# Overwriting the sorted rows with pad rows early, by copies inside DRAM, in a two-pass mixture-of-experts kernel

## The chip, the cores and the metric

The kernel runs on one core of a Trainium2 chip. The core has TensorE (PE), VectorE (DVE), ScalarE (ACT), GpSimd (POOL) and SyncE (SP), each with its own instruction queue, and 16 DMA engines that all queues share. SP's and ACT's transfers are issued by hardware queues of their own (q1 and q10 in the profile), POOL's by a software queue (q0). The metric is device time in microseconds (us).

## The reference

The input x is 2 x 1024 rows of 128 numbers. Three layers with residuals, the first and the last the same mixture-of-experts feed-forward with the same weights:

```python
x = x + 0.5 * ffn(layernorm(x))
x = x + attn(layernorm(x))      # projections, short convolutions, delta rule, gate, output
x = x + 0.5 * ffn(layernorm(x))

def ffn(x):                     # 8 experts, each token goes to one
    pb = softmax(xf @ gate_w + gate_b)
    weights = pb * (one-hot of the largest)
    for e in range(8):
        h = gelu(xf @ w1[e] + b1[e])
        out += weights[:, e] * (h @ w2[e] + b2[e])
```

## The kernel before

The program is a row of blocks: the first feed-forward (`moe_ffn`, rep 0), the attention layer in three blocks (`attn_project`, `attn_delta`, `attn_mix`), and the second feed-forward (`moe_ffn`, rep 1). Each block gives every engine its list of work, in the order in which it is written; all engines meet at a barrier at the block's end, SP too.

A feed-forward sorts the 2,048 tokens by expert. `xsort` is a tensor in DRAM with eight regions of CAP = 16 x 128 + 128 = 2,176 rows, one for each expert, and 128 rows behind them; a row is 258 floats (1,032 bytes): the normalised token, its number, its weight, and the row that the result is added to. The 128 rows behind the regions hold pad rows: zeros, with a token number of 2,048, which the final scatter drops.

DVE and PE work out each token's expert and its rank in it, in four chunks of four tiles, and with them the row `pos`. POOL then scatters each tile of `xr` to `xsort` with an indirect DMA (L201), 16 of them. An expert's tokens don't fill its last tile of 128 rows, so pad rows must stand behind them. `store_pads` does that: when all the counts are known, DVE copies them to `padrow` (L448), and SP (even experts) and ACT (odd experts) each read four of them into a register (L153) and store the 128-row tile `pad` behind the last token (L154). POOL makes `pad` (L190 to L192). In the first feed-forward `lead["store_pad"]` also stores one pad tile behind the regions (L1937).

SP waits for all scatters and all pads and then loads the 23 sorted tiles in turn, each from a row that it reads from `row0` (L177, L178):

```python
sp.wait_ge(scattered, 16 * NT)
sp.wait_ge(pads_in, 16 * NE)
```

PE turns a tile (`turn_rows`, L273), multiplies it by the first weights (`up`, L282) and the second (`down`, L292); ACT copies and applies gelu (L346, L354), DVE copies the expert's weights to `w1s` (L475) and takes the result (L486), POOL scatters it (L208). Before its loop ACT copies the biases into the weights (L340), and it does so behind its pad stores.

In the projection block neither SP nor ACT issues a transfer, and SP has no work at all. In the mixing block SP issues 16 loads: four pieces of `m_wpair` (L1374) and twelve of `m_pairs` (L1378 to L1380), which PE's gate waits for (L1426): the first ten of them for the first half of the sequence. In the second feed-forward SP first issues the two loads of the weights (L162, L163).

Of the kernel before, what the change touches and what calls it, by code (L numbers as in the profile page):

```python
# [6 lines left out]
I32 = mybir.dt.int32  # L7
# [40 lines left out]
def moe_ffn(nc, rep, cst, mem, banks, NT, NE, F, lead=None):  # L48
# [19 lines left out]
    with ExitStack() as ctx:  # L68
# [87 lines left out]
        with nc.Block() as block:  # L156

            @block.sync
            def _(sp):
                if rep == 0:  # L160
                    lead["load_x"](sp)
                sp.dma_start(W1[:, :, 0:F], a["L0_ffn_w1"].rearrange("e d f -> d e f")).then_inc(weights_in, 16)  # L162
                sp.dma_start(W2[:], a["L0_ffn_w2"].rearrange("e (j f) d -> f e j d", f=P)).then_inc(weights_in, 16)  # L163
                if rep == 0:
                    sp.wait_ge(pad_made, 1)
                    lead["store_pad"](sp, pad)
                store_pads(sp, range(0, NE, 2))

                sp.wait_ge(row0_ready, 1)
                first_rows = [sp.value_load(row0[0:1, t:t + 1], min_val=0, max_val=NE * CAP) for t in range(2)]  # L170
                sp.wait_ge(scattered, 16 * NT)
                sp.wait_ge(pads_in, 16 * NE)
                if rep == 0:
                    sp.wait_ge(mem["pad_stored"], 16)
                for c, (g, n) in enumerate(LOADS):
                    for t in range(g, g + n):
                        r = first_rows[t] if t < 2 else sp.value_load(row0[0:1, t:t + 1], min_val=0, max_val=NE * CAP)  # L177
                        sp.dma_start(xs[:, t, :], xsort[bass.ds(r, P), :]).then_inc(x_loaded[c], 16)  # L178
                if rep == 0:
                    lead["load_attn"](sp)  # L180

                sp.wait_ge(y_stored, 16 * MAXT)
                if not last:
                    xnext = mem["xnext"].rearrange("(t p) d -> p t d", p=P)
                    for c in range(NC):
                        sp.dma_start(X[:, tiles(c), :], xnext[:, tiles(c), :]).then_inc(mem["x_back"][c], 16)

            @block.gpsimd
            def _(gp):
                gp.memset(pad[:, 0:D], 0.0)  # L190
                gp.memset(pad[:, D:D + 1].bitcast(I32), NT * P)
                gp.memset(pad[:, D + 1:WIDE], 0.0).then_inc(pad_made, 1)  # L192
                if rep == 0:
                    lead["gpsimd"](gp)
                gp.iota(base[:, 0, :], [[CAP, NE]], base=0, channel_multiplier=0, allow_small_or_imprecise_dtypes=True).then_inc(ranks_read, 1)
                if rep == 0:
                    gp.wait_ge(mem["numbered"], 1)
                for c in range(NC):
                    gp.wait_ge(pos_ready, c + 1)
                    for t in range(c * CT, (c + 1) * CT):  # L200
                        gp.indirect_dma_start(xsort, bass.IndirectOffsetOnAxis(pos[:, t:t + 1], 0),  # L201
                                              xr[:, t, :], None).then_inc(scattered, 16)
                if rep == 0:
                    lead["make_masks"](gp)
                for t in range(MAXT):
                    gp.wait_ge(y_ready, t + 1)

                    gp.indirect_dma_start(mem["out"] if last else mem["xnext"], bass.IndirectOffsetOnAxis(row(t), 0), Y[:, t, :], None,  # L208
                                          bounds_check=NT * P - 1, oob_is_err=False).then_inc(y_stored, 16)
# [98 lines left out]
            @block.scalar  # L308
            def _(act):
                if rep == 0:  # L310
                    lead["scalar"](act)
                def root(c):
                    act.wait_ge(var_ready, c + 1)
                    act.activation(rstd[:, tiles(c)], vare[:, tiles(c)], ACT.Sqrt).then_inc(std_ready, 1)

                def copy_turned(c):
                    act.wait_ge(xnT_psum, c + 1)
                    act.activation(XNT[:, c * BANK:(c + 1) * BANK], pT[c % 2][:], ACT.Copy).then_inc(xnT_ready, 1)  # L318

                def exp(c):  # L320
                    act.wait_ge(shifted, c + 1)
                    act.activation(ex[:, tiles(c), :], lg[:, tiles(c), :], ACT.Exp).then_inc(exp_done, 1)

                root(0)
                copy_turned(0)
                root(1)
                exp(0)
                copy_turned(1)
                root(2)
                exp(1)  # L330
                copy_turned(2)
                root(3)
                exp(2)
                copy_turned(3)
                exp(3)
                store_pads(act, range(1, NE, 2))
                if rep == 0:
                    lead["take_bias"](act)
                act.wait_ge(mem["bias_ready"], 3)
                act.activation(W1[:, :, F:F + FC], b1T[:], ACT.Copy).then_inc(b1_ready, 1)  # L340
                if rep == 0:
                    lead["take_taps"](act, 0, 3)

                def copy_rows(t):
                    act.wait_ge(xT_psum, t + 1)
                    act.activation(xT[:, t, :], pX[t % 2][:, 0:P], ACT.Copy).then_inc(xT_ready, 1)  # L346

                def gelu(t):
                    act.wait_ge(h_psum, t + 1)
                    if t >= 2:  # L350

                        act.wait_ge(y_psum, t - 1)
                    for j in range(FC):
                        act.activation(hT[:, t % 2, j, :], pH[t % 2][:, j * P:(j + 1) * P], ACT.Gelu,  # L354
                                       bias=w1s[:, t % NB, F + j:F + j + 1]).then_inc(h_ready, 1)

                copy_rows(0)
                copy_rows(1)
                for t in range(MAXT):
                    gelu(t)  # L360
                    if t + 2 < MAXT:
                        copy_rows(t + 2)
                if rep == 0:
                    lead["take_products"](act)
                    act.wait_ge(var_ready, NC + 1)
                    act.activation(rstd[:], vare[:], ACT.Sqrt).then_inc(std_ready, 1)
                    lead["take_taps"](act, LASTQ, LASTQ + 1)

            @block.vector
            def _(ve):  # L370
# [74 lines left out]
                place(3)  # L445

                ve.wait_ge(ranks_read, NC + 1)
                ve.tensor_copy(padrow[:], base[:, NC, :]).then_inc(padrow_ready, 1)  # L448
                ch.step(ve.tensor_tensor(cnt[:], base[:, NC, :], base[:, 0, :], ALU.subtract))
                ch.step(ve.tensor_tensor(over[:], cnt[:].unsqueeze(2).to_broadcast([P, NE, NT]),  # L450
                                         cst["tilestart"][:, 0:NT].unsqueeze(1).to_broadcast([P, NE, NT]), ALU.is_gt))
# [76 lines left out]
def attn_project(nc, cst, mem, banks, B, L, NH, done):  # L528
# [7 lines left out]
    with ExitStack() as ctx:  # L536
# [37 lines left out]
            return ap.rearrange("p (t c) -> p t c", c=P)  # L574

        with nc.Block() as block:

            @block.tensor
            def _(pe):
# [1448 lines left out]
```

## Time and profile before

| | us |
|---|---|
| three runs | 508.62, 513.08, 515.13 |
| their median | 513.08 |
| the profiled execution, its time | 509.69 |
| its span, from first to last instruction | 507.7 |
| PE busy in it | 411.1 (81%) |
| DVE busy | 303.5 (60%) |
| ACT busy | 239.8 (47%) |
| POOL busy | 143.3 (28%) |
| moved by DMA | 30.31 MB |

A row of the timeline gives the start, the duration, the engine and the line, and in brackets how long the engine was idle before it and what released it; SPq and ACTq are the queues that issue transfers, and their duration is that of the issue. Landing times stand apart, in the chain of waits and in the list of issues. A packet is one piece of a transfer on one DMA engine.

### The profile page before, as it was taken

To read this page: it belongs to the slowest core of one execution; us is meant where nothing else is said; L and a number is where in the kernel's file an instruction comes from. 1 tells how busy PE (TensorE), PEld (TensorE's weight loads), DVE (VectorE), ACT (ScalarE), POOL (GpSimd) and SP (SyncE) were. 2 spreads that over 40 slices of the span, in tenths; PEclk is the share of its full clock that TensorE was granted. 3 is DMA by queue.
4 is the path that set the end of the run, shared out by engine and by line. 5 is a ranking of instruction groups with operands and counts; after the bars stand their busy time and mean duration, and the time that the engine had idled before them with its cause. 6 is when DMAs were issued, how large, how long until landed. Compare 5 with 4: busy or idle time off the path is not lost. (4 is left out here: it accounts for less than half of the span.)

```text
span 507.7 us, 13213 instructions
## 1 busy us (share of the span) xinstructions
PE 411.1 (81%) x5049; PEld 327.3 (64%) x5049; DVE 303.5 (60%) x818; ACT 239.8 (47%) x511; POOL 143.3 (28%) x172
## 2 busy tenths in 40 slices
PE   2756999979987989889999999965999537329995
PEld 1655999766566877667777666752445426319994
DVE  5943455367684588778765555462278867714551
ACT  2605676466681587976421000052655336116763
POOL 4467355400002396030100000030024203713553
PEclk9999999969896599999999999997898555558998
DMA  7726442120000000000000000038000019344400
GB/s 258 222 95 156 132 126 63 44 67 1 1 0 4 4 4 4 6 4 4 2 3 1 0 1 1 3 74 196 1 0 1 1 44 327 128 126 133 118 32 4
DMA packets 27388, 30.31 MB, mean 60 GB/s; under 512 B 7670, under 2 KB 20899, under 8 KB 27328
## 3 DMA queue, kind: packets, MB, share of 16 engines
q1 hardware_dynamic: 22672, 22.04, 16.0%
q0 software_dynamic: 3008, 6.34, 3.8%
q10 hardware_dynamic: 1648, 1.10, 0.8%
q8 instruction: 41, 0.67, 0.5%
q14 instruction: 19, 0.16, 0.1%
HBM read 17.48 MB, written 9.49 MB: 53 GB/s over the span
## 5 line engine op out<-in xcount | busy, mean ns | idle before, releaser
L354 ACT ACTIVATE hT<-bank,w1s 128x128 f32<-128x128 f32 x184 | 52.5, 368 | 27.4 <-PE bank L282 27.4
L282 PE MATMUL bank<-xT,w1s 128*128 128x128 f32 x368 | 52.4, 289 | 0.6 <-ACT xT L346 0.6
L292 PE MATMUL bank<-W,hT 128*128 x368 | 50.2, 281 | 0.8 <-ACT hT L354 0.8
L282 PEld LDWEIGHTS bank<-xT,w1s 128*128 128x128 f32 x368 | 48.1, 204 | 1.1 <-ACT xT L346 1.0
L292 PEld LDWEIGHTS bank<-W,hT 128*128 128x128 f32 x368 | 46.3, 198 | 1.2 <-issue 1.2
L1240 DVE TENSOR_TENSOR d_BD<-bank,quarter 128x2048 f32<-128x2048 f32 x16 | 36.6, 2289 | 11.3 <-PE bank L890 11.3
L475 DVE COPY w1s<-W 128x516 f32 x46 | 20.6, 450 | 36.4 <-issue 29.1
L1102 ACT ACTIVATE d_BD<-d_TP 32x512 f32<-32x512 f32 x64 | 40.5, 633 | 0.9
L201 POOL DMA_INDIRECT xsort<-xr,pos x32 | 31.5, 984 | 32.9 <-DVE pos L424 24.4
L208 POOL DMA_INDIRECT out<-Y,xs x23 | 22.6, 983 | 35.2 <-issue 18.7
L486 DVE SCALAR_TENSOR_TENSOR Y<-bank,xs 128x128 f32<-128x128 f32 x46 | 16.2, 351 | 27.0 <-PE bank L292 17.9
L208 POOL DMA_INDIRECT xnext<-Y,xs x23 | 22.6, 982 | 25.9 <-issue 18.9
L1573 POOL TENSOR_TENSOR m_DSQ<-DEL 128x512 f32<-128x512 f32 x4 | 4.1, 1039 | 91.4 <-POOLq L897 89.9
L1294 DVE TENSOR_TENSOR d_TT<-bank,blk 128x128 f32<-128x128 f32 x64 | 16.5, 292 | 18.1 <-PE bank L1039 18.1
L273 PE MATMUL bank<-ident,xs 128*128 128x128 f32 x46 | 13.5, 298 | 15.4 <-DMA xs<-xsort 15.2
L1139 ACT ACTIVATE d_TMP<-bank 128x512 f32<-128x512 f32 x4 | 2.4, 597 | 48.7 <-PE bank L1073 48.7
L220 PE MATMUL bank<-ident,xr 128*128 128x128 f32 x32 | 9.9, 464 | 17.8 <-DVE xr L384 16.4
L1024 PE MATMUL bank<-d_TT,KBT 128*32 128x128 f32 x128 | 20.1, 279 | 4.6 <-DVE d_TT L1294 3.7
L890 PE MATMUL bank<-d_BD,d_ATP 128*32 128x128 f32 x512 | 18.4, 287 | 5.2 <-ACT d_BD L1102 5.2
L1039 PE MATMUL bank<-xr,K 32*128 32x128 f32 x128 | 22.6, 296 | 0.0
L1289 DVE TENSOR_TENSOR xr<-xr,bank 32x128 f32<-32x128 f32 x64 | 16.2, 284 | 10.2 <-PE bank L1024 10.2
L1580 POOL TENSOR_TENSOR m_PM<-DEL,m_ex 128x512 f32<-128x512 f32 x4 | 6.3, 1578 | 51.8 <-DVE m_ex L1633 51.8
(298 smaller groups left out, 967.0 us busy)
## 6 DMA issues: line engine op xcount, KB each, us to landing
xs<-xsort SPq DMA_DIRECT2D x46, 129.0 KB, 2.1
W<-in_L_ffn_w SPq DMA_DIRECT2D x2, 2048.0 KB
xsort<-pad SPq DMA_DIRECT2D x9, 129.0 KB
xsort<-pad ACTq DMA_DIRECT2D x8, 129.0 KB
xr<-in_L_attn_x SPq DMA_DIRECT2D x4, 256.0 KB, 5.1
xr<-xnext SPq DMA_DIRECT2D x4, 256.0 KB, 3.9
m_pairs<-FS SPq DMA_DIRECT2D x4, 256.0 KB, 5.0
m_pairs<-firT SPq DMA_DIRECT2D x4, 256.0 KB, 4.9
```

What stands on the lines that cost most here:

```text
L201: gp.indirect_dma_start(xsort, bass.IndirectOffsetOnAxis(pos[:, t:t + 1], 0), xr[:, t, :], None).then_inc(scattered, 16)
L208: gp.indirect_dma_start(mem["out"] if last else mem["xnext"], bass.IndirectOffsetOnAxis(row(t), 0), Y[:, t, :], None, bounds_check=NT * P ...
L282: mm = pe.matmul(pH[t % 2][:, j * P:(j + 1) * P], w1s[:, t % NB, j * P:(j + 1) * P], xT[:, t, :], start=True, stop=True)
L292: mm = pe.matmul(pY[t % 2][:, 0:D], hT[:, t % 2, j, :], W2[:, bass.ds(e, 1), j, :], start=(j == 0), stop=(j == FC - 1))
L354: act.activation(hT[:, t % 2, j, :], pH[t % 2][:, j * P:(j + 1) * P], ACT.Gelu, bias=w1s[:, t % NB, F + j:F + j + 1]).then_inc(h_ready, 1)
L475: ve.tensor_copy(w1s[:, t % NB, :], W1[:, bass.ds(experts[t], 1), :]).then_inc(staged, 1)
L890: mm = pe.matmul(bank[a * C:(a + 1) * C, t * P:(t + 1) * P], lhs(t, a), BD[:, slot, t * NH + a, :], start=True, stop=True)
L1024: pe.matmul(banks[b][c * C:(c + 1) * C, 0:P], WT[:, cols], SB[:, b, :], start=True, stop=True).then_inc(ws_psum, 1)
L1039: pe.matmul(banks[2 + b][:, 0:P], K[rows, tile, :], U[rows, tile, :], start=(n == 0), stop=(n == STEPS_S - 1), skip_group_check=True).then ...
L1102: cp = act.activation(spread_dst(i % 2, a), blocks(TP[a * C:(a + 1) * C, i % NG, :]), ACT.Copy)
L1240: ve.tensor_tensor(BD[:, 2 + i % 2, :, :].rearrange("p s (a n) -> p s a n", n=C), all_blocks(banks[i % 2][:]), mask, ALU.mult).then_inc(z_ ...
L1294: ve.tensor_tensor(SB[:, b, :], banks[2 + b][:, 0:P], cst["blk"][:], ALU.mult).then_inc(s_ready, 1)
```

## The change

In the second feed-forward no pads are stored behind the counts, `pad` is not made again and `padrow` is not written. Instead SP issues eight copies in the projection block. Each overwrites one expert's region of 2,176 rows with the 128 pad rows that stand behind the regions, 17 times over. Their completion counts on `pad_stored`, and POOL waits for all of it before its first scatter in the second feed-forward. The code views a region as 17 x 16 pieces of 8 rows.

```diff
@@ moe_ffn, sync
-                store_pads(sp, range(0, NE, 2))
+                if rep == 0:
+                    store_pads(sp, range(0, NE, 2))
...
                 sp.wait_ge(scattered, 16 * NT)
-                sp.wait_ge(pads_in, 16 * NE)
                 if rep == 0:
+                    sp.wait_ge(pads_in, 16 * NE)
                     sp.wait_ge(mem["pad_stored"], 16)
@@ moe_ffn, gpsimd
-                gp.memset(pad[:, 0:D], 0.0)
-                gp.memset(pad[:, D:D + 1].bitcast(I32), NT * P)
-                gp.memset(pad[:, D + 1:WIDE], 0.0).then_inc(pad_made, 1)
                 if rep == 0:
+                    gp.memset(pad[:, 0:D], 0.0)
+                    gp.memset(pad[:, D:D + 1].bitcast(I32), NT * P)
+                    gp.memset(pad[:, D + 1:WIDE], 0.0).then_inc(pad_made, 1)
                     lead["gpsimd"](gp)
...
+                if rep == 1:
+                    gp.wait_ge(mem["pad_stored"], 16 + 16 * NE)
                 for c in range(NC):
@@ moe_ffn, scalar
-                store_pads(act, range(1, NE, 2))
                 if rep == 0:
+                    store_pads(act, range(1, NE, 2))
                     lead["take_bias"](act)
@@ moe_ffn, vector
-                ve.tensor_copy(padrow[:], base[:, NC, :]).then_inc(padrow_ready, 1)
+                if rep == 0:
+                    ve.tensor_copy(padrow[:], base[:, NC, :]).then_inc(padrow_ready, 1)
@@ attn_project, a block of its own for sync
+            @block.sync
+            def _(sp):
+                xsort, cap = mem["xsort"], NT * P + P
+                n = xsort.shape[0] // cap
+
+                def pieces(ap):
+                    return ap.rearrange("(a b) w -> a (b w)", b=8)
+
+                empty = pieces(xsort[n * cap:n * cap + P, :])
+                for e in range(n):
+                    sp.dma_start(xsort[e * cap:(e + 1) * cap, :].rearrange("(n a b) w -> n a (b w)", b=8, a=P // 8),
+                                 empty.unsqueeze(0).to_broadcast([cap // P] + list(empty.shape))).then_inc(mem["pad_stored"], 16)
```

On SP, the order of the program before from the end of the first feed-forward to the mixing stage's loads (the line, the operation, the tensors, the shape that the instruction carries):

```order
L156 UNCONDITIONAL_BRANCH
L1369 UNCONDITIONAL_BRANCH
L1374 DMA m_wpair<-wbr 64x2x128 x4
L1378 DMA m_pairs<-FS 64x1024
L1379 DMA m_pairs<-firT 64x1024
L1380 DMA m_pairs<-VP 64x1024
```

The same place of the program after, whose line numbers are 12 to 17 higher:

```order
L156 UNCONDITIONAL_BRANCH
L582 UNCONDITIONAL_BRANCH
L592 DMA xsort<-xsort 17x3x11008 x8
L580 UNCONDITIONAL_BRANCH
L1386 UNCONDITIONAL_BRANCH
L1391 DMA m_wpair<-wbr 64x2x128 x4
L1395 DMA m_pairs<-FS 64x1024
L1396 DMA m_pairs<-firT 64x1024
L1397 DMA m_pairs<-VP 64x1024
```

The eight copies stand ahead of the mixing stage's loads in the same queue, and the shape of each is 17 x 3 x 11,008 floats: the sixteen pieces of 8 rows, which lie one behind the other, stand as three pieces of 44,032 bytes.

On SP in the second feed-forward, the program before, from the weights to the first sorted tile:

```order
L162 DMA W_1<-in_L_ffn_w 128x8x512
L163 DMA W_1<-in_L_ffn_w 128x32x128
L153 TENSOR_LOAD padrow
L153 ISA x2
L154 ISA
L154 DMA xsort<-pad 128x258
```

```order
L170 TENSOR_LOAD row_1
L170 ISA x2
L170 TENSOR_LOAD row_1
L170 ISA x2
L178 ISA
L178 DMA xs<-xsort 128x258
```

And after:

```order
L162 DMA W_1<-in_L_ffn_w 128x8x512
L163 DMA W_1<-in_L_ffn_w 128x32x128
L171 TENSOR_LOAD row_1
L171 ISA x2
L171 TENSOR_LOAD row_1
L171 ISA x2
L179 ISA
L179 DMA xs<-xsort 128x258
```

The four pad stores with their register loads are gone between the weights and the first sorted tile.

## Rows read from the trace of the kernel before

**Rows 1.** The page: the span, and DMA busy share in 40 slices, in tenths.

```profile
span 507.7 us, 13213 instructions
...
DMA  7726442120000000000000000038000019344400
```

**Rows 2.** Waits of SP's queue in the whole span: waiting line, releaser, us, times, longest.

```profile
SPq L897 <- PEq L897: 180.9, 1, 180.9
SPq L1367 <- PEq L1367: 64.3, 1, 64.3
SPq L576 <- PEq L576: 43.6, 1, 43.6
```

**Rows 3.** Timeline: start us, us, engine, line, operation, count, idle before and its releaser.

```profile
110.88 0.09 DVE L752 MEMSET a_PRE<- 128x6 f32 x2 [0.97 <-PEq L156]
...
347.90 2.04 PE L1426 MATMUL bank<-XNT,w1x 128*128 128x512 f32 x2 [5.81 <-DMA m_pairs<-VP]
```

**Rows 4.** Chain that ended last, second feed-forward: start us, us, what.

```profile
449.71 2.10 DMA xsort<-pad
...
452.57 2.16 DMA xs<-xsort
```

**Rows 5.** Timeline around the head of the second feed-forward's loop.

```profile
445.48 0.96 POOL L201 DMA_INDIRECT xsort<-xr,pos  x1 [0.30 <-issue]
...
448.93 0.23 ACT L340 ACTIVATE W<-b1T 128x32 f32<-128x32 f32 x1 [11.73 <-issue]
450.37 0.43 DVE L475 COPY w1s<-W 128x516 f32 x1 [6.86 <-issue]
```

**Rows 6.** Queue and issues of ACT: queue, packets; out<-in, count, KB each.

```profile
q10 hardware_dynamic: 1648, 1.10, 0.8%
...
xsort<-pad ACTq DMA_DIRECT2D x8, 129.0 KB
...
gw<-in_L_ffn_gate_w ACTq DMA_DIRECT2D x1, 4.0 KB
gb<-in_L_ffn_gate_b ACTq DMA_DIRECT2D x1, 4.0 KB
b1rows<-in_L_ffn_b ACTq DMA_DIRECT2D x1, 16.0 KB
b2rows<-in_L_ffn_b ACTq DMA_DIRECT2D x1, 4.0 KB
c_firp<-in_L_attn_fir_l ACTq DMA_DIRECT2D x1, 15.5 KB, 5.4
```

**Rows 7.** Windows: stretch us, busy of each engine, clock, DMA share, GB/s.

```profile
0.00:16.74 16.74, 6.96 (x28) 5.87 (x28) 10.11 (x52) 6.22 (x10) 6.22 (x27) 1.00 0.86 267
...
421.00:423.00 2.00, 1.37 (x5) 0.85 (x5) 1.86 (x10) 0.40 (x2) 0.00 (x0) 0.50 1.05 401
423.00:425.00 2.00, 2.00 (x10) 2.00 (x11) 1.41 (x10) 1.95 (x4) 0.00 (x0) 0.50 1.06 305
...
449.00:451.00 2.00, 0.00 (x0) 0.00 (x0) 0.43 (x1) 0.16 (x1) 0.00 (x0) 0.50 0.58 198
```

**Rows 8.** DMA issues of the mixing stage: count, KB each, us to landing.

```profile
m_pairs<-FS SPq DMA_DIRECT2D x4, 256.0 KB, 5.0
m_pairs<-firT SPq DMA_DIRECT2D x4, 256.0 KB, 4.9
m_pairs<-VP SPq DMA_DIRECT2D x4, 256.0 KB, 5.1
...
m_wpair<-wbr SPq DMA_DIRECT2D x4, 64.0 KB, 2.1
```

**Rows 9.** Timeline of SP's queue at the start of the kernel.

```profile
3.69 2.47 SPq L163 DMA_DIRECT2D W<-in_L_ffn_w  x1
6.21 10.53 SPq L1937 DMA_DIRECT2D xsort<-pad  x1
```

## The prediction

> **What bounds the kernel now.** I read the page first: a span of 507.7 us, and a DMA row that is 7 to 9 tenths busy at both ends and nearly 0 in the middle [rows 1]. Then the waits of SP's queue, because the change puts work there. SP waits 43.6 us in the projection, 180.9 us in the delta stage and 64.3 us in the mixing stage [rows 2]; with the first instruction of the projection at 110.88 us [rows 3] these make stage borders of about 110.9, 154.5 and 335.4 us. So during 225 us neither SP nor the DMA engines have anything to do, and copies that the DMA engines finish in that time would be free. Last I read the chain that ended last, at the second feed-forward. PE's first transpose there waits for the first load of a sorted tile, and that load waits for the last pad store: the store takes 2.10 us from 449.71 (landing 451.81), the load 2.16 us from 452.57 [rows 4]. Behind it PE runs 23 tiles without a gap to the end. Only that short head can be gained.
>
> **Removed: the pads behind the counts.** The second feed-forward loses 4 pad stores on SP and 4 on ACT, the copy of `padrow`, 3 memsets on POOL, and SP's wait on `pads_in`. What SP waits for next is `scattered`. POOL's last scatter stands at 445.48 and takes 0.96 us, so it is issued at 446.44 [rows 5]. No row shows when a scatter has landed; the nearest is the pad store's 2.10 us, a write of the same tensor, and I take it: 448.54. Before, SP went on at 451.81, so it gains 3.3 us. The bounds: 5.4 us if a scatter landed at once, nothing if it takes as long as 5.4 us. The other two things that PE's first tile needs don't take the place of the load. ACT's copy of the biases (L340, 448.93) stood behind ACT's own four stores and moves ahead with them, and DVE's first `w1s` copy (450.37) was behind that [rows 5]. The memsets and the `padrow` copy cost nothing on the path: POOL is idle then until its first scatter, and DVE has nothing late in front of it. The loop itself is unchanged. **-3.3 us.**
>
> **Added: eight copies inside DRAM.** Each writes 17 x 128 rows of 1,032 bytes, that is 2.246 MB; eight make 17.97 MB. What decides is how many DMA engines share them. The order list gives their shape as 17 x 3 x 11008: the 16 pieces that the code asks for have been merged again, and the outer dimension is 17. What the trace tells of outer dimensions: ACT's queue issued thirteen transfers: `gw`, `gb`, `c_firp` and eight pads with 128 rows each, `b1rows` with 32 and `b2rows` with 8 [rows 6]. Their rows sum to 11 x 128 + 32 + 8 = 1,448 packets; the queue's row says 1,648. The other 200 are 12 x 16 + 8. I read that as one closing packet on each engine that a transfer uses: sixteen engines for every transfer whose outer dimension is a multiple of 16, eight for the one with 8 rows. All are equal shares. Seventeen can't be cut into equal shares over 2 to 16 engines, so my forecast is that each copy runs on **one** engine, and all eight on the same one. Rows alone leave the other reading open (rows dealt out in turn, the seventeenth to the first engine again), for no transfer here has an outer dimension above 16 that isn't a multiple of 16.
>
> The Trainium skill ("DMA: Bandwidth & Descriptors", section on why a DMA increments its semaphore by 16 and not by 1) decides between the two: the engine count is the largest number up to 16 that divides the slowest dimension of both sides, and on these queues it is the lowest-numbered engines that are used. By that rule the count here is 1 and the time is that of the forecast; by rows dealt in turn it would be that of the first rival below. No run so far shows a 17.
>
> The price on one engine. When the weights stream in 2 KB rows, all sixteen move 401 GB/s [rows 7], 25.1 GB/s each. 17.97 MB at 25.1 GB/s are **717 us**, from 110.9 to 827.6 us. The trace has no copy inside DRAM, so bounds: the same weights in 512-byte rows move at 305 GB/s or less, and the pads at 198 GB/s with 0.58 of the engines busy, 21.3 GB/s for a busy one [rows 7], which gives 843 us. The other way: 512 bytes at 305/16 GB/s take 26.9 ns, 2,048 at 25.1 take 81.7 ns; the straight line through these goes at 28.0 GB/s for long pieces, 642 us. I take 25.1, the rate that was seen.
>
> **What waits for it.** Two things. POOL's first scatter of the second feed-forward now waits for `pad_stored` at 144. But something earlier does: the 16 loads of the mixing stage (4 `m_wpair` of 64 KB, 12 `m_pairs` of 256 KB [rows 8]) go through SP's queue too, and on the first engine their share stands behind the copies. PE's first gate matmul (L1426, 347.90) is the one that waits for them [rows 3]. Ahead of it are 4 x 64 KB and 6 x 256 KB; a sixteenth is 0.11 MB, 4.6 us at 25.1 GB/s. It then starts at 827.6 + 4.6 = 832.2 instead of 347.9: **+484.3 us**. POOL's wait has by then been over, so it adds nothing.
>
> **Does SP itself get stuck?** It must hand over all eight before the barrier at the projection's end. SP's issue of the first pad store took from 6.21 to 16.74 us [rows 9]. The delta stage then runs 180.9 us to 754, still ahead of 827.6: it is hidden under the last 145 pieces, and the mixing stage waits for its loads. The other queues (instruction fetches, the scatters) are nearly idle in that time.
>
> **Sum:** 507.7 + 484.3 - 3.3 = 988.7 us of span; with the 2.0 us that the profiled execution's own time (509.69) has around its span, **991 us**. The median of the runs before, 513.08, is 3.4 us above that execution.
>
> **The rivals.**
> (1) The copies are spread over all engines, so the kernel isn't slower. For it: the 8-row transfer is as well explained by dealing rows in turn. At 401 GB/s the eight take 45 us; with the seventeenth row on one engine 2/17 of 17.97 MB at 25.1 GB/s is 84 us, to 195 us, and both are over long before 335.4. Only -3.3 us is left: 506 us. That is also what it would be with eight or more engines in use; the point from which it decides is 335.4 - 110.9 = 224.5 us, reached with 717 / 224.5 = 3.2 engines. Chance 0.17.
> (2) One engine, and the delta stage is not hidden. If the 44,032-byte pieces are cut to 4 KB, 94 of them are only 0.39 MB. The eighth copy is taken at 110.9 + 7 x 89.6 - 15.4 = 723 us, the delta stage ends at 904, and the rest follows: 904 - 335.4 = +568.6, or 1,075 us in all. At the slower rate of 21.3 GB/s (105.4 us a copy) the same working gives 1,183; without the cutting it is 953.9 + 5.4 - 347.9 = +611, 1,118 us. For it: no packet of SP's queue so far is as long as 8 KB. Against it: the shape itself was cut to 44,032 bytes. Chance 0.20.
> (3) The change doesn't do what it says: SP's wait was not the pads' but the scatters'. Then the head gains nothing, 3.3 us more in either case. It changes no chance.
>
> **How the numbers follow.** One engine with the delta stage hidden: 0.63; (2) 0.20; (1) 0.17. Faster by over 2% needs 10 us, which the head of the second feed-forward doesn't hold: 0.01. Within 2% (what a measurement of this kernel can tell from no change): 0.16. Slower: 0.83. The range starts at the fast line, 642 us in place of 717, 915 us, and ends at (2) with the slower rate, 1,185 rounded. The likeliest case's own range is 915 to 1,118.
>
> **What would show it.** Right: SP's wait in the projection vanishes while its eight issues last some 460 us; the mean DMA busy share is about 1/16 for some 700 us at 25 GB/s; the longest wait of PE is for `m_pairs` at L1426; the first tile load of the second feed-forward follows the last scatter. Wrong: 17.97 MB moved by 200 us at 200 GB/s or more, and a projection of 43.6 us as before. Then the reading of the 200 packets fails at 17, and everything behind it.

## The result: 940 us, and the profile after

| | before | after |
|---|---|---|
| median of the runs, us | 511.96 | 939.84 |
| the profiled execution, us | 509.69 | 939.81 |
| its span, us | 507.7 | 937.8 |

The median before is now that of four executions. The ratio is 1.833, with a 95% interval of 1.823 to 1.843 (that of the two medians is 1.836). Some executions of one kernel show a lower mean clock than others and are a few per cent longer; ratios and intervals in this document compare the faster ones alone. The forecast was 991 us, from 915 to 1,185. The kernel got slower by the mechanism that was put first, and 51 us less than it said.

The page of the kernel after, its span, the DMA row and the rate in 40 slices (it answers to [rows 1]), and the queue that holds SP's transfers:

```profile
span 937.8 us, 13167 instructions
...
PE   4599895000000000000006988999960006966497
...
DMA  8352100000000000000000000000011222006340
GB/s 248 127 136 72 52 27 27 28 26 28 26 28 26 28 26 26 28 26 28 26 28 29 30 33 30 30 27 30 27 39 37 58 60 64 1 0 201 108 121 17
...
q1 hardware_dynamic: 22512, 39.48, 12.9%
```

For fourteen slices of 23.4 us on end PE is idle, and all that time the DMA engines move 26 to 28 GB/s. Windows of the same execution (columns as in [rows 7]) give the mean, and the share of the sixteen engines that was busy:

```profile
113.00:500.00 387.00, 39.52 (x173) 23.86 (x172) 32.62 (x48) 28.89 (x44) 0.00 (x0) 0.55 0.06 27
500.00:690.00 190.00, 173.16 (x3626) 138.98 (x3627) 114.88 (x216) 72.47 (x118) 35.51 (x19) 0.88 0.07 30
...
776.00:777.00 1.00, 0.00 (x0) 0.00 (x0) 0.00 (x0) 0.00 (x0) 0.00 (x0) 0.50 1.00 194
```

0.06 of sixteen is one engine. The last of the copies' pieces is done at about 776 us; by then all sixteen engines are busy with the last of the mixing stage's loads. The queue's packets say the same in another way. Before there were 22,672 of them:

```profile
q1 hardware_dynamic: 22672, 22.04, 16.0%
```

The change takes 4 pad stores of 128 + 16 packets from SP's queue, which leaves 22,096, and there are 22,512: 416 more, or eight copies of 51 pieces and **one** closing packet each.

What waited (SP's queue first, as in [rows 2], then all engines):

```profile
SPq L914 <- PEq L914: 191.0, 1, 191.0
SPq L1384 <- PEq L1384: 72.2, 1, 72.2
...
SPq L580 <- PEq L580: 0.2, 1, 0.2
```

```profile
PE bank L926 <- PEq L580: 346.3, 1, 346.3
...
PE bank L1443 <- DMA m_pairs<-VP: 84.3, 1, 84.3
```

SP has no wait left in the projection (0.2 us, where there were 43.6). PE waits 346.3 us at the barrier in front of the delta stage, and 84.3 us in front of the gate. SP's queue from the timeline:

```profile
111.30 388.81 SPq L592 DMA_DIRECT2D xsort<-xsort  x8
691.92 10.44 SPq L1391 DMA_DIRECT2D m_wpair<-wbr  x4
...
703.05 25.28 SPq L1396 DMA_DIRECT2D m_pairs<-firT  x1
728.37 12.94 SPq L1397 DMA_DIRECT2D m_pairs<-VP  x1
```

```profile
782.91 2.05 PE L1443 MATMUL bank<-XNT,w1x 128*128 128x512 f32 x2 [84.34 <-DMA m_pairs<-VP]
```

```profile
880.32 1.07 POOL L204 DMA_INDIRECT xsort<-xr,pos  x1 [0.30 <-issue]
...
883.22 6.39 SPq L179 DMA_DIRECT2D xs<-xsort  x7
...
885.51 0.93 PE L276 MATMUL bank<-ident,xs 128*128 128x128 f32 x2 [11.62 <-DMA xs<-xsort]
```

The same places of the second feed-forward before:

```profile
415.24 0.38 SPq L162 DMA_DIRECT2D W<-in_L_ffn_w  x1
...
452.02 24.87 SPq L178 DMA_DIRECT2D xs<-xsort  x23
```

The gate starts at 782.91 in place of 347.90, +435.0 us. From the issue of the second feed-forward's weights to its first tile load are 32.9 us (850.29 to 883.22), before 36.8, and to the end 87.5, before 92.5. 507.7 + 435.0 - 5.0 = 937.7: the whole difference is accounted for.

### The profile page after: what moved, and what is told of

Read it like the earlier page. It is cut to its first block and busy times, and to the rows that moved or that the text cites. A ratio compares the mean times of both kernels' runs of the same rounds, so it can differ in the third digit from the quotient of the medians.

```text
span 937.8 us, 13167 instructions
## 1 busy us (share of the span) xinstructions
PE 421.7 (45%) x5049; PEld 334.4 (36%) x5049; DVE 304.2 (32%) x817; ACT 239.6 (26%) x511; POOL 143.4 (15%) x169
## 3 DMA queue, kind: packets, MB, share of 16 engines
q1 hardware_dynamic: 22512, 39.48, 12.9%
## 5 line engine op out<-in xcount | busy, mean ns | idle before, releaser
L926 PE MATMUL bank<-KBT,KT 32*32 32x32 f32 x512 | 8.2, 237 | 346.5 <-PEq L580 346.3
L926 PEld LDWEIGHTS bank<-KBT,KT 32*32 32x32 f32 x512 | 7.5, 150 | 346.9 <-issue 346.8
L1213 DVE TENSOR_TENSOR d_TMP<-d_ATP,t2mask 128x512 f32<-128x512 f32 x4 | 2.8, 692 | 353.3 <-ACT d_ATP L1111 353.3
L1111 ACT ACTIVATE d_ATP<-bank 128x512 f32<-128x512 f32 x4 | 2.4, 597 | 358.8 <-PE bank L926 358.8
L1160 POOL MEMSET d_BD<- 128x4096 f32 x1 | 3.5, 3511 | 401.5 <-SPq L914 401.5
L1443 PE MATMUL bank<-XNT,w1x 128*128 128x512 f32 x16 | 10.5, 744 | 84.3 <-DMA m_pairs<-VP 84.3
L1443 PEld LDWEIGHTS bank<-XNT,w1x 128*128 128x128 f32 x16 | 2.9, 223 | 86.1 <-issue 86.1
L1610 DVE TENSOR_REDUCE ST<-m_FSt 128x16 f32<-128x512 f32 x4 | 2.7, 680 | 88.0 <-ACT m_FSt L1497 88.0
L1497 ACT ACTIVATE m_FSt<-bank 128x512 f32<-128x512 f32 x4 | 2.4, 590 | 91.3 <-PE bank L1410 91.2
## 6 DMA issues: line engine op xcount, KB each, us to landing
m_pairs<-firT SPq DMA_DIRECT2D x4, 256.0 KB, 16.7
```

The lines of the kernel that those rows point to most:

```text
L926: mm = pe.matmul(banks[6 + g % 2][h * C:(h + 1) * C, t * P + c * C:t * P + (c + 1) * C], KT[rows, cols], KBT[rows, cols], start=True, stop ...
L1443: pe.matmul(bank[:], cst["w1x"][:], XNT[:, cols], start=True, stop=False)
```

## The experiments

### Sixteen outermost

```diff
-                    return ap.rearrange("(a b) w -> a (b w)", b=8)
+                    return ap.rearrange("(a b) w -> a (b w)", a=16)
...
-                    sp.dma_start(xsort[...].rearrange("(n a b) w -> n a (b w)", b=8, a=P // 8),
-                                 empty.unsqueeze(0).to_broadcast([cap // P] + list(empty.shape))).then_inc(mem["pad_stored"], 16)
+                    sp.dma_start(xsort[...].rearrange("(n a b) w -> a n (b w)", n=cap // P, a=16),
+                                 empty.unsqueeze(1).to_broadcast([16, cap // P, empty.shape[1]])).then_inc(mem["pad_stored"], 16)
```

> The changed kernel with one thing different: each copy is viewed as 16 x 17 pieces of 8 rows (8,256 bytes), 16 outermost, instead of 17 x 3 pieces of 44,032 bytes. My theory (the DMA engines of a transfer are the largest number up to 16 that divides its outer dimension, so 17 gives one engine and 16 gives sixteen): 17.97 MB at 16 x 27.06 GB/s (the rate of one engine in the changed kernel: 408 pieces in 664 us) are 42 us, perhaps 90 if copies inside DRAM share a limit, over by about 155 to 200 us of the span, long before the mixing stage. SP isn't held, the gate waits for nothing, and only the head of the second feed-forward is left: 3.9 to 5.0 us less than before, a span of 502.7 to 503.8, a time near 505. The queue's packets grow to 22,096 + 8 x (16 x 17 + 16) = 24,400. Rival (the slowness lies in copies inside DRAM or in their number of bytes, not in the shape): 700 us or more. Rival (the copies disturb the projection's or the delta stage's own work): those stages longer than 43.6 and 180.9 us.

Measured: 516.39 us (509.20 to 523.28), a ratio to before of 1.0136 with an interval of 0.9993 to 1.028. The same bytes, the same place, the same number of transfers, and the time is 423 us shorter: it was the shape of the transfers alone. The order of the dimensions changed, and with it the length of a piece (8,256 bytes in place of 44,032); the versions with 34 and 68 outermost, both with pieces of 33,024 bytes, tell these two apart. The packets are 24,400, as expected.

```profile
PEclk9999999968975599999688999997988755557999
...
GB/s 263 205 156 112 140 101 74 83 198 322 327 316 224 4 4 4 4 5 4 1 2 1 1 1 1 1 8 203 54 0 1 1 0 294 142 103 133 101 31 4
...
q1 hardware_dynamic: 24400, 39.48, 25.1%
```

The copies run at 316 to 327 GB/s and are over in some 60 us. But it isn't the 505 us that I expected. The profiled execution (522.2 us) is one of the longer ones, and its delta stage takes 197.6 us, before 180.9. Windows of its beginning, and of the same stretch of the kernel before:

```profile
151.10:171.10 20.00, 10.45 (x402) 9.85 (x402) 4.19 (x6) 1.45 (x3) 3.51 (x1) 0.50 0.59 226
171.10:191.10 20.00, 19.61 (x612) 16.51 (x615) 14.72 (x16) 13.35 (x22) 13.22 (x7) 0.68 0.02 4
```

```profile
154.50:174.50 20.00, 17.30 (x580) 16.12 (x580) 8.49 (x13) 6.40 (x11) 5.34 (x2) 0.56 0.02 4
174.50:194.50 20.00, 18.02 (x698) 14.40 (x690) 17.14 (x14) 16.75 (x28) 19.29 (x11) 0.93 0.01 4
```

In the first 20 us of the stage PE gets 10.5 us of work done where it got 17.3, and the clock is still at its lower level for most of the next 20. What PE waited for there, in the kernel with 16 outermost and before:

```profile
PE bank L926 <- issue: 9.3, 3, 7.3
```

```profile
PE bank L909 <- issue: 2.2, 1, 2.2
```

It waited for nothing that the profile shows ("issue"; I read it as waiting for its own instructions), once for 7.3 us, while the last of the copies kept the DMA engines 0.59 busy in that window. This is a cost that I had put at nothing; see the last two experiments. It isn't all of the stage's 16.7 us. By the count of matmuls done, the stage is some 9 us behind after its first 40 us and 11 us after 60; the rest comes later, where the granted clock dips to 0.86, 0.80 and 0.91 in three windows of 20 us. The changed kernel, with one engine of copies, has such a dip too (0.79 and 0.70), and the kernel before has none in its profiled execution, so that part can't be put down to wide copies.

### The sixteen-wide copies, and the pads still stored

The same kernel, with the pads of the second feed-forward stored behind the counts as before (each of the two queues first waits for the copies; `pad`, `padrow` and the wait on `pads_in` are back too).

```diff
 moe_ffn, sync and scalar
-                if rep == 0:
-                    store_pads(...)
+                if rep == 1:
+                    eng.wait_ge(mem["pad_stored"], 16 + 16 * NE)
+                store_pads(...)
```

> One part alone: the sixteen-wide copies are made in the projection, and the second feed-forward still stores its pads behind the counts, as before. Theory: the copies cost nothing where they are, so this is the time of the kernel before within 1 us, and all of the gain of the kernel without pads comes from their absence. Rival (copies slow the attention stages by their traffic): some us slower than before.

Measured: 519.88 us (511.38 to 526.21), ratio 1.0178, interval 0.9964 to 1.0393. Not settled within 1 us; what can be read is the stages. The head of the second feed-forward is 35.9 us from weights to first tile load, with the pads gone 33.4. The delta stage takes 197.5 us, without the pads 197.6, and PE has "issue" waits here too in its first 60 us (8.3 us; without the pads 10.8, before 3.1). So the pads' absence gives back 2.5 to 3.9 us at the head (the second from the changed kernel against the kernel before), and the delta stage beside or behind the copies was longer by more than that in both profiled executions, which are both among the longer ones of their kernels.

### Thirty-four outermost

```diff
-                empty = pieces(xsort[n * cap:n * cap + P, :])
+                empty = xsort[n * cap:n * cap + 64, :].rearrange("r w -> (r w)")
...
+                    sp.dma_start(xsort[...].rearrange("(n r) w -> n (r w)", r=64),
+                                 empty.unsqueeze(0).to_broadcast([cap // 64, empty.shape[0]])).then_inc(mem["pad_stored"], 16)
```

> Each copy as 34 x 2 pieces of 33,024 bytes, 34 outermost. Theory (largest divisor up to 16): 34 gives two engines. 8.98 MB on each at 27.06 GB/s are 332 us, from 111.3 to 443.6. About 118 pieces were outstanding on the engine when the changed kernel's eighth copy was taken; with 34 pieces per engine and copy the eighth is taken after 7 x 34 - 118 = 120 pieces of 1.22 us, at 258 us, so the delta stage starts then instead of at 154.5, ends at 439 to 449, and the gate's loads land by 450 to 462: span 605 to 617, time 607 to 619. The queue's closing packets: 2 a copy, so 22,096 + 8 x (68 + 2) = 22,656. Rival (rows are dealt out in turn and 17 was one engine for some other cause): 16 engines, about 505 us, 22,096 + 8 x (68 + 16) = 22,768 packets.

Measured: 683.35 us, a span of 681.3.

```profile
GB/s 271 149 142 145 73 87 32 55 54 54 54 54 54 54 54 54 54 54 55 58 58 57 59 58 54 52 1 1 0 2 152 50 0 1 25 271 102 139 69 11
...
q1 hardware_dynamic: 22656, 39.48, 18.1%
```

```profile
107.50 212.16 SPq L589 DMA_DIRECT2D xsort<-xsort  x8
513.52 2.67 SPq L1388 DMA_DIRECT2D m_wpair<-wbr  x4
```

Two engines it is: 54 GB/s, twice one engine's, and 22,656 packets, two closing ones a copy. Rows dealt out over sixteen engines are excluded, with 17 and with 34. The time is 64 us above the upper end of what I expected (619 us), and the timeline shows why: SP was held for 212 us, not some 150. The delta stage starts at 319.7, ends 194 us later at 513.5, and there the loads find an empty queue. 513.5 - 335.4 = +178.1, less 4.1 for the second feed-forward: 681.7.

### Sixty-eight outermost

```diff
-                empty = xsort[n * cap:n * cap + 64, :].rearrange("r w -> (r w)")
+                empty = xsort[n * cap:n * cap + 32, :].rearrange("r w -> (r w)")
```

This is against the version with 34; the destination has `r=32`.

> Each copy as 68 pieces of 33,024 bytes, 68 outermost. Theory (largest divisor up to 16): four engines, 4.49 MB on each, 166 us from 111.3 to 277. SP isn't held (17 pieces per engine and copy, seven copies are 119), and 277 is before the mixing stage at 335.4: about 505 us, since four engines are more than the 3.2 at which the copies begin to show. 22,096 + 8 x (68 + 4) = 22,672 packets. Rival (dealt over sixteen): the same time but 22,768 packets; so the packets tell, and the DMA busy share of about 4/16 for 166 us against 16/16 for 42 us.

Measured: 535.71 us, a span of 533.8.

```profile
GB/s 261 205 167 94 150 89 61 80 80 107 101 109 109 111 113 113 113 114 110 114 84 1 1 1 1 1 2 73 184 1 0 1 1 178 216 92 129 136 31 4
...
q1 hardware_dynamic: 22672, 39.48, 23.2%
```

```profile
108.45 69.44 SPq L589 DMA_DIRECT2D xsort<-xsort  x8
366.29 2.69 SPq L1388 DMA_DIRECT2D m_wpair<-wbr  x4
```

Four engines, 111 GB/s, 22,672 packets: right. The time was not (about 505 expected): SP was held for 69 us, so the projection ended at 177.9 instead of about 151. The copies were done before the mixing stage, as expected, and it still cost 27 us at a barrier.

### Four copies on one engine, four on sixteen

The first four copies keep 17 outermost, the other four have 16 outermost.

```diff
-                for e in range(n):
+                for e in range(n // 2):
...
+                for e in range(n // 2, n):
```

> Four copies as in the changed kernel (17 outermost) and then four with 16 outermost. This tells apart the two things that can hold the program: SP at the barrier, and the mixing stage's loads behind the copies. The first engine has 4 x 51 pieces of 44,032 bytes (332 us) and then 4 x 17 of 8,256 (21 us): it is done at 464 us. If only the loads' place in the queue mattered, the gate would start at 470 in place of 347.9: 507.7 + 122 - 5 + 2 = 627 us. If SP also stands at its eighth copy until no more than about 118 pieces are left on the first engine (255 - 118 = 137 pieces, 223 us), the projection's barrier opens at 334, the delta stage ends at 515 to 525 and the mixing stage runs from there: 682 to 694 us. Theory: the second.

Measured: 783.69 us, a span of 781.8.

```profile
107.61 57.64 SPq L592 DMA_DIRECT2D xsort<-xsort  x4
165.31 257.47 SPq L599 DMA_DIRECT2D xsort<-xsort  x4
614.46 2.66 SPq L1398 DMA_DIRECT2D m_wpair<-wbr  x4
```

The loads' place behind the copies alone would give 627 us; the measured time is 157 us above it, so the barrier decides here. It is also some 90 us above the 682 to 694 that I had expected with the barrier. SP hands over its eighth copy at 422.8. By then the first engine, busy from 109 us on, has done 313.8 / 1.62 = 194 of the 255 pieces that stand ahead of the eighth (1.62 us a piece: below): 61 are left, not the 118 of my expectation. With that the sum closes to 0.7 us: mixing stage at 614.5, +279.1, less 4.3 for the second feed-forward, 782.5, where the span is 781.8.

### The changed copies, and the pads still stored

The edit of the second experiment, on the changed kernel itself: 17 outermost, and

```diff
-                if rep == 0:
-                    store_pads(...)
+                if rep == 1:
+                    eng.wait_ge(mem["pad_stored"], 16 + 16 * NE)
+                store_pads(...)
```

> The changed kernel's copies, unchanged (17 outermost), and the second feed-forward still stores its pads behind the counts. Theory: all of the loss is the copies', and the pads' absence gave back 4 to 5 us, so this takes 939.8 + 5 = 945 us. Rival (the second feed-forward was shorter for another cause, the clock or the emptier DMA queues): 940.

Measured: 939.70 us, where I expected 945. It reads like the rival, the same time as the changed kernel, but isn't it. From the weights' issue to the end it takes 91.6 us, the changed kernel 87.5, before 92.5: the 4.1 us are there. The first feed-forward of this execution happened to be 3.3 us shorter (the copies start at 108.03, in the changed kernel at 111.30), and as everything hangs on the copies' end, that is taken off the total: 937.8 + 4.1 - 3.3 = 938.6, where the span is 937.9. The head alone: 36.5 us to the first tile load with pads, 32.9 without.

### The mixing stage's loads on ACT's queue

In outline:

```diff
 attn_mix: the loop over m_wpair and m_pairs moves from the sync block
-                        sp.dma_start(...)
 to the head of the scalar block
+                act.dma_start(...)
```

> The changed kernel's copies (17 outermost, SP's queue), but the sixteen loads of the mixing stage are issued by ACT, on its own queue. If the place behind the copies in one queue is what holds the gate, the loads now only take turns with the copies on the first engine. With one piece in turn the 56 pieces of the first ten loads there wait 1.63 us each, 91 us from 692: no gain, 940 us. With more than one piece in turn, the gate starts near 710, and the second feed-forward near 777, where its first scatter finds the copies done: 860 to 870 us. If the gate waited for something else (POOL, the barrier), 940 as well, but then with the loads landed early. ACT spends some 12 us on the issues.

Measured: 935.59 us.

```profile
776.72 2.05 PE L1430 MATMUL bank<-XNT,w1x 128*128 128x512 f32 x2 [53.13 <-DMA m_pairs<-VP]
```

```profile
DMA to landing us min/median/max: 4.2/6.1/86.7
```

The gate starts at 776.72, 670 us after the first copy, in the changed kernel 672. The copies start 4.6 us earlier here (106.66), which is the 4 us of the total. The slowest load takes 86.7 us to land: it is the tenth of those that the gate waits for, issued at 689.85. The median of 6.1 us doesn't say that half of the loads were complete so early. The ten share one semaphore, and each adds 16 to it. If that is one from each of its sixteen closing packets, fifteen engines that are done with all ten make a count of 150, which passes the 144 of nine loads, and only the tenth shows when the first engine has done its shares. That the copies were nearly over by then (their end lies a few microseconds before) would leave two readings, but the packets decide: from 722 to 770 us SP's queue moves 28 of them and ACT's queue 28, and nothing else moves. The shared engine takes one piece of each queue in turn, a 1.6 us piece of a copy for each small one of a load (my estimate by that was 91 us). So another queue doesn't help, and the question which of the two, the queue or the engine, holds the loads has this answer: the engine is enough. The other fifteen engines had done their shares of the ten long before: the DMA busy share is 0.99 from 692 to 696 us and 0.05 from 704 to 708. What the gate's start would be with loads that keep off the copies' engine wasn't run.

### Four engines, in two blocks

All copies are viewed as `"(n a b) w -> a n (b w)"` with `a=4`. In outline:

```diff
 attn_project, sync
+                for e in range(0, 4):
 attn_delta, a block for sync
+                for e in range(4, 8):
```

> A version that could beat both: 4 outermost in each copy, so four DMA engines, with four of the copies issued in the projection block and the other four in the delta block. With 68 pieces outstanding on an engine when the next pair of copies is taken (seen in every run so far), four copies of 17 pieces hand over at once, so no barrier waits; 8 x 20.8 us of copying end by about 111 + 83 and 152 + 83 + some, long before the mixing stage; and twelve of the sixteen engines stay free for instruction fetches. Theory: projection 43 us, delta stage as before (181 to 186 us), second feed-forward 3.3 us shorter at its head; about 3 us faster than the kernel before of the same rounds, which is less than its own spread (501 to 519 us in the last rounds). Rival (any copy traffic beside the delta stage costs time): a delta stage of 190 us or more and no gain.

Measured: 510.87 us (505.98 to 519.08), a ratio of 1.0015 with an interval of 0.9964 to 1.0065: no difference that can be measured. The projection is about 44 us again and no barrier waits:

```profile
107.91 2.85 SPq L592 DMA_DIRECT2D xsort<-xsort  x4
151.96 24.95 SPq L926 DMA_DIRECT2D xsort<-xsort  x4
346.94 2.67 SPq L1405 DMA_DIRECT2D m_wpair<-wbr  x4
```

The delta stage of the profiled execution (518.07 us, one of the longest of twelve) takes 195 us, where I expected 181 to 186 and the rival 190 or more. Its "issue" waits in the first 60 us are 4.5 us, 1.4 us more than before. By the count of matmuls the stage is some 3 us behind after 60 to 80 us; the other 11 come later, where the granted clock falls to 0.79 and 0.67 in two windows of 20 us (before it stayed at 1.00). Whether the copies have a part in that dip isn't shown. The best version of this change thus gives about what it costs.

### Sixteen-wide copies beside the delta stage

In outline:

```diff
 attn_project
-            @block.sync: the eight copies
 attn_delta
+            @block.sync: the eight copies, with a=16 outermost
```

> The sixteen-wide copies, all eight issued in the delta block instead of the projection. In the kernel with 16 outermost, the copies still ran for the first 17 us of the delta stage; PE stood there 7.3 and 1.8 us for nothing but its own instructions, the clock rose at 184 instead of 177 us, and the stage took 197.6 us instead of 180.9. Theory (the fetches of PE's instructions wait behind the copies on the same DMA engines, and that keeps the clock low): with all of the 58 us of copying beside PE's 3,600 short matmuls the stage takes 25 to 45 us longer than 180.9, the span is 530 to 550 us, and PE's stalls put down to issue lie all in the first 60 us of the stage. Rival (the longer stage is the clock's own wandering from run to run): 181 to 198 us.

Measured: 541.05 us, a span of 539.2, a delta stage of 220 us.

```profile
152.00:172.00 20.00, 10.97 (x447) 10.32 (x433) 6.29 (x9) 1.79 (x3) 2.76 (x1) 0.55 0.85 312
172.00:192.00 20.00, 10.79 (x254) 8.60 (x255) 7.39 (x7) 9.32 (x15) 12.54 (x7) 0.67 0.85 317
192.00:212.00 20.00, 14.09 (x333) 10.35 (x336) 8.52 (x9) 8.77 (x15) 13.07 (x6) 0.67 0.73 275
```

```profile
PE bank L927 <- issue: 12.5, 3, 4.5
PE bank L894 <- issue: 8.5, 3, 4.1
PE bank L967 <- issue: 2.9, 1, 2.9
```

PE's "issue" waits in the first 60 us of the stage are 23.9 us, before 3.1. The clock rises and falls with them: in windows of 2 us it is at 1.00 from 182 to 184, from 188 to 190 and from 200 to 204, each time PE then stands idle (0.00 busy in 182:184, 190:192 and 204:206), and the clock is back at 0.50 by 186, 192 and 206. Only when the copies have gone, from 212 us, does it stay up for 40 us. The stage lost 39 us: by the count of matmuls some 26 in its first 60 us, beside the copies, and the rest later, most of it in the dip of the stage's middle (0.78, 0.63 and 0.83), which the changed kernel has too. The rival, wandering of the clock alone, would have ended at 198.

### Eight outermost

```diff
-                    return ap.rearrange("(a b) w -> a (b w)", b=8)
+                    return ap.rearrange("(a b) w -> a (b w)", a=8)
```

The destination is viewed as in the first experiment, with `a=8`.

> Eight outermost, all copies in the projection: 2.25 MB on each of eight engines, 83 us at 27.06 GB/s, so from 108 to 191 us. SP takes the eighth copy when 68 of 119 pieces of 0.61 us are left, after 31 us: no barrier waits. 22,096 + 8 x (136 + 8) = 23,248 packets. Theory of the fetches: a fetch waits only if it is on one of the eight busy engines, so the delta stage's first 40 us lose less than the sixteen-wide kernel's first 17: a stage of 183 to 192 us, a span of 507 to 516. Rival (fetches wait wherever copies run): the stage takes over 200 us, since the copies lie beside it for 40 us instead of 17.

Measured: 519.30 us, a span of 517.3, a delta stage of 198.1 us.

```profile
GB/s 266 205 164 105 150 95 74 83 102 207 215 215 216 213 212 27 4 4 5 1 2 1 1 0 1 2 1 154 112 0 1 1 0 226 192 101 126 133 31 4
...
q1 hardware_dynamic: 23248, 39.48, 23.9%
```

Eight engines, 215 GB/s, 23,248 packets. On the stage it is between my two readings. PE's "issue" waits in the stage's first 60 us, over all runs:

| copies beside them | "issue" waits, us |
|---|---|
| none (before) | 3.1 |
| one engine (changed kernel, its version with pads, loads on ACT) | 1.7, 2.4, 3.5 |
| two engines | 3.0 |
| four engines | 4.5, 4.9 |
| sixteen for 8 us, then one (four copies on each) | 7.1 |
| eight for 40 us | 9.6 |
| sixteen for 17 us (without and with pads) | 10.8, 8.3 |
| sixteen for 60 us | 23.9 |

The version with four copies on one engine and four on sixteen shows both in one execution: one wait of 5.1 us while the DMA engines are 0.76 to 0.79 busy, and 2.0 us in all in the rest of the 60, when one engine is left. So wide traffic makes PE wait, and traffic on one to four engines hardly does. That it is the fetch of PE's instructions that waits is my reading, and isn't shown. In the first 60 us of its delta stage the sixteen-wide kernel of the experiment above moved 8 packets through the instruction queue (q8), and they took 0.9% of the engines' time, 1.1 us for each; in the kernel before there were 15 in 1.6%, 1.0 us for each. So a fetch that is under way is hardly slower, and the wait would have to lie in front of it, where no row looks.

## Why the prediction was right, point by point

**One engine.** Right, and shown by six shapes: outer dimensions 17, 34, 68, 8 and 16 gave 1, 2, 4, 8 and 16 closing packets a copy, and rates of 27, 54, 111, 215 and some 320 GB/s. The outer dimension 4 of the split version closes with 4 as well (111 GB/s). The step that was least sure in the prediction, from an 8-row transfer to one with 17, holds; rival (1) is excluded for this shape. The Trainium skill's rule ("DMA: Bandwidth & Descriptors", why a DMA increments its semaphore by 16 and not by 1) named 1 for 17, and the trace agrees, as it does in every run with another shape.

**The price.** The mechanism was right and the size was off: 717 us, measured 665 (111.3 to about 776). The issues of the eight copies, as the trace lists them (min, median and max in ns):

```profile
L592 SPq DMA_DIRECT2D xsort<-xsort x8: 627/724/164885, 111.3 to 499.5; - x8
```

The longest, 164.9 us, is the time of exactly two copies, 4.491 MB: 27.2 GB/s for one engine, where I had taken 25.1 from the weights' 2 KB rows. The straight line through the two row sizes, which I used as a bound only, said 28.0. For pieces of 44 KB the line was the better guess: 1.62 us each instead of 1.76. This term made the forecast 52 us too high; the others nearly cancel (0.4 us for the start, 2.3 for the loads, 1.7 the other way for the second feed-forward).

**The loads.** Right. 4.6 us forecast between the copies' end and the gate, measured about 7.

**The hold of SP.** The mechanism was right, the term was not. I had one threshold: the next transfer is taken when 94 pieces are left. The trace shows steps: in the changed kernel the copies are taken in pairs, two at once, a third after 55 us and a fourth with it, then two more after 165 us and again after 165 us. At each step about 68 pieces are left on the engine from the copies taken before, and the eighth is taken with the seventh, at 500.1 instead of 573. In the changed kernel this changed nothing (the delta stage was hidden either way, and PE then waited 84 us for the gate). It misled me in three expectations: I had replaced 94 by 118 from the same trace, counting the eighth as if it had been taken alone. With 34 pieces a copy about 65 were left at the eighth, in the mixed kernel 61. What exactly a ring holds, and why the first pads of the program waited for 94 small rows, stays open.

**The delta stage** took 191.0 us, forecast 180.9. The time went to the clock: beside a single engine of copies PE's "issue" waits were no longer than before, but the granted clock fell to 0.79 and 0.70 in two windows in its middle. It cost nothing here. By the count of matmuls 1 us of the 10 was lost in the first 60 us and the rest in that dip; the same copies with the pads stored had a stage of 185.4 us, so it is no fixed price of the copies.

**The head of the second feed-forward.** Right: forecast -3.3 us. In nine kernels without the pads the first tile load is issued 32.9 to 33.4 us after the weights (mean 33.1), in the three with them 35.9 to 36.8 (mean 36.4). SP goes on 1.7 us after POOL is done with the last scatter (881.39 to 883.1), which I read as its landing, where I took 2.1. The other 1.1 us of the 5.0 in the changed kernel came behind the head; from run to run this part spreads from 54.6 to 58.1 us, about as much as the whole gain.

**The rivals.** (2) didn't come true: the pieces weren't cut to 4 KB (51 a copy by the packets), and the rate was above, not below. (3), the scatters holding SP instead of the pads, is excluded by the head.

**What I costed at nothing and wasn't.** Copies on many engines beside a stage of many short matmuls. The prediction called the fetches nearly idle and priced rival (1) at 506 us; the kernel that makes it true takes 516 in the median (its ratio to before lies between 0.9993 and 1.028, so no gain is shown and a small loss isn't excluded).

## What to carry to other kernels

Look at the shape that the instruction carries, not the one that the code wrote: here dimensions that lie one behind the other were merged, and an outermost broadcast of 17 put each transfer on one DMA engine. Put a dimension of 16 outermost when the transfer must be quick, and count the closing packets to see how many engines a transfer got. And a background transfer isn't free because its queue is idle: it can hold the issuing engine at the next barrier, every later load that shares its engine, and, when it is wide, the engine that it was to run beside.

## What I had not expected of the hardware

SP's queue took transfers in steps: with 51 pieces each, two at once, two more after 55 us, and then two more every two copies (164.9 us), with 61 to 68 pieces left on the engine in all runs. An engine that two queues share took one piece of each in turn, whatever their sizes (28 packets of either in 48 us). PE lost 23.9 us to "issue" in 60 us beside copies at 312 and 317 GB/s on all engines, and 1.7 us beside copies on one engine at 27 GB/s. Copies inside DRAM ran at 27.2 GB/s on one engine and at some 320 GB/s on sixteen, so sixteen together reached about three quarters of sixteen times one. And the kernel before itself spreads from 501.4 to 518.6 us on one chip, with a mean granted clock of 0.894 and 0.865 at these ends: a gain of 3 us in one stage can't be told from the kernel's time, only from the stage.
